# A graph network on one core: the first team's source slots sorted by readiness, 64 columns gathered ahead of a round's last stores, and the node groups in another order

## The chip, the cores and the metric

One core of one Trainium2 chip. The metric is the device time of one execution in microseconds (us). Engine names as in the profile: PE (TensorE matmul), PEld (its weight load), DVE (VectorE), ACT (ScalarE), POOL (GpSimd), SP (SyncE, which here only issues DMAs and passes semaphores on).

## The reference, cut to what matters

6250 nodes, 106250 edges sorted by target; the last edge of each node is its own loop. Three rounds of a mixture of experts (MoE) over the mean of the neighbours, then two attention layers (GAT) over the same edges.

```
h = x @ W_in + b_in                                   # 6250 x 256
for l in range(3):                                    # MoE rounds
    agg = segment_sum(h[src], dst) / deg
    logits = concat([h, agg]) @ router_W[l] + router_b[l]
    gates = softmax over the top 2 of 8 experts
    weak = relu(agg @ weak_W[l] + b)                  # 4 experts, 256 x 256
    strong = relu(agg @ strong_W1[l] + b) @ strong_W2[l] + b   # 4 experts, 256 x 512 x 256
    h = h + sigmoid(h @ conf_W[l] + conf_b[l]) * sum_e gates[e] * experts[e]
x = layernorm(x + h @ W_out + b_out)
x = layernorm(x + gat(elu(gat(x))))                   # softmax over each node's edges, 4 heads, then 1
```

A round cannot read h[src] of a node before the round before it has stored that node's new h.

## The kernel before, in words

**Groups, slots, teams.** Nodes are ranked by degree, the highest first, and cut into 49 groups of 128 (one node per partition). A group is as wide as its highest degree: that many *slots*, or columns. Column c of a group is one gathered row per partition. The 798 columns of all groups stand in one list (filled up to 800). Four groups are a team; 12 teams and a last one of one group. Which rank-group comes where is set by `rank_i`: group (rank-group + 1) * 12 mod 49. With the inputs of the reference this makes the teams 44, 62, 79, 69, 62, 75, 60, 61, 75, 56, 59, 74 and 22 columns wide (worked out from the drawn edges by the kernel's own rule).

**Gathering (POOL).** Per column POOL issues one indirect DMA (L591) of 128 rows of `hidden_tab[r]` (MoE rounds, 1 KB a row) or `gat_tab` (attention) into `ring`, a buffer of 32 columns. The row numbers are in `stage`, which SP loads by 32 columns. Four columns are a unit. SP waits for each unit's DMAs (L418) and raises `arrived`; DVE raises `ring_free` as it consumes a unit, and POOL waits for that before it writes over it. At the end of a round POOL waits for `table_done`, all 13 stores of the new h (L617).

**Summing and the MoE (DVE, PE, ACT).** `aggregate(r, q, j)` on DVE sums a group's columns: the first unit masked (L884), whole units added (L890), the last masked (L894), own row (L898), four slots to one (L901), times 1/degree (L905). In `step(q)` DVE sums the four groups of team q+1 between the pieces of team q: `rank_experts`, `weigh_experts`, `add_weak` (L934, L938) and `add_strong` (L925). PE begins team q by transposing its four sums (L1655, which waits for `agg_ready`), then runs router, strong and weak experts. ACT takes the results out of PSUM. `add_strong` of the last strong expert raises `h_done`; ACT then stores the team (`keep_state`, L1380). So a team's step on PE can begin when all columns of the team have come and been summed and PE is through with the team before.

**Between rounds.** After the last team, PE and ACT make the own part of the router's logits for all teams (L1633, L1644, L1307), and SP loads the next round's weights, after the first 32 columns of the round have come and PE's last strong expert is done (L443 to L448).

**Round 0** also notes for each gathered row where its node stands in the sorted order (`note_places`, L862), from which the list `place_tab` for all later rounds is made.

## Time and profile before

| | |
|---|---|
| median of 3 runs | 5833.66 us (5831.72 to 5834.1) |
| span of the profiled execution | 5830.9 us; no other time of it is recorded |
| busy: PE, PEld, DVE, ACT, POOL | 3215.0, 2026.1, 3413.5, 1201.4, 4155.7 us |
| first gather of MoE rounds 0, 1, 2 | 304.12, 1416.55, 2521.92 us |
| first gather of attention layers 1, 2 | 3698.28, 4739.33 us |

The span is 2.8 us below the median of the runs. Times in rows are us from the span's start. A gather counts as busy for its 0.95 us on POOL; the 0.30 us between two gathers is POOL's own issue time and shows as idle "<-issue".

### The profile page before, as it was taken

How to read it: one execution, taken by the hardware profiler on the slowest of the kernel's cores; microseconds unless marked ns; L12 is line 12 of the kernel's file. 1: busy time of each engine (PE TensorE's matmuls, PEld its weight loads, DVE VectorE, ACT ScalarE, POOL GpSimd, SP SyncE). 2: the span in 40 equal slices, each digit the busy share in tenths (PEclk: the TensorE clock that was granted, in tenths of full speed). 3: DMA queues.
4: the chain of work that ended last, by engine and by line, in shares of the span. 5: the costliest groups of instructions: out<-in, count | busy, mean ns of one | idle time of the engine just before them, and what ended most of it. 6: DMA issues, size and time to landing. Idle time of an engine off the chain costs nothing.

```text
span 5830.9 us, 59667 instructions
## 1 busy us (share of the span) xinstructions
PE 3215.0 (55%) x11995; PEld 2026.1 (35%) x11995; DVE 3413.5 (59%) x6741; ACT 1201.4 (21%) x2737; POOL 4155.7 (71%) x4323
## 2 busy tenths in 40 slices
PE   4088899999879899989899999200000000000000
PEld 3064555557545555565565566200000000000000
DVE  3255766773657666536566665555565556566563
ACT  1022323333223333323333333200000000000000
POOL 7777777772777777557777766477777767777777
PEclk8579999998889999979999999655555555555555
DMA  4244444441443333233333332222222222222221
GB/s 110 78 138 108 113 113 110 109 109 49 144 108 111 110 109 109 80 114 105 101 104 99 103 96 65 56 59 59 59 59 59 59 46 55 55 56 56 55 56 50
DMA packets 249575, 500.72 MB, mean 86 GB/s; under 512 B 104203, under 2 KB 133444, under 8 KB 249050
## 3 DMA queue, kind: packets, MB, share of 16 engines
q0 software_dynamic: 176592, 446.04, 29.6%
q1 hardware_dynamic: 56234, 33.56, 2.2%
q10 hardware_dynamic: 16608, 19.67, 0.9%
q14 instruction: 105, 0.86, 0.1%
q8 instruction: 36, 0.59, 0.0%
HBM read 464.21 MB, written 34.76 MB: 86 GB/s over the span
## 4 chain that ended last, share of the span: by engine, by line
POOL 25%; PE 22%; issue 16%; DVE 14%; DVEq 13%; DMA 5%; ACT 2%; SPq 1%; ACTq 0%; POOLq 0%
POOL ring L591 22%; PE ps_w1a L1681 4%; PE ps_w1b L1681 4%; PE ps_gate L1706 3%; DMA ring<-gat_tab,stage 3%; PE ps_wide L1706 3%; DVE ps_wide L1139 3%; PE ps_weak_a L1693 2%; PE ps_weak_b L1693 2%; DMA ring<-hidden_tab,stage 2%; DVEq L887 2%; DVE ps_wide L934 2%; DVEq L1171 1%; DVEq L1181 1%; DVEq L1184 1%
## 5 line engine op out<-in xcount | busy, mean ns | idle before, releaser
L591 POOL DMA_INDIRECT ring<-hidden_tab,stage x2400 | 2306.3, 961 | 955.5 <-issue 889.6
L591 POOL DMA_INDIRECT ring<-gat_tab,stage x1600 | 1539.3, 962 | 589.4 <-issue 545.5
L890 DVE TENSOR_TENSOR ps_wide<-ps_wide,ring 128x1024 f32<-128x1024 f32 x450 | 557.8, 1240 | 209.1 <-SPq L418 125.4
L1681 PE MATMUL ps_w1a<-agg_team_t,wbuf 128*128 128x512 f32 (+1 forms) x1248 | 561.6, 572 | 7.3 <-ACT strong L1347 5.9
L1706 PE MATMUL ps_gate<-wbuf,strong 128*128 128x256 f32 x2400 | 559.9, 379 | 0.0
L1810 PE MATMUL ps_w1a<-ident,agg_team_t 128*128 128x128 f32 x28 | 7.8, 434 | 995.0 <-DVE agg_team_t L1217 995.0
L1681 PE MATMUL ps_w1b<-agg_team_t,wbuf 128*128 128x512 f32 (+1 forms) x1248 | 556.0, 568 | 0.0
L1706 PE MATMUL ps_wide<-wbuf,strong 128*128 128x256 f32 x2304 | 537.2, 379 | 0.0
L1706 PEld LDWEIGHTS ps_gate<-wbuf,strong 128*128 128x128 f32 x2400 | 432.6, 190 | 111.2 <-issue 47.7
L1499 ACT ACTIVATE ps_gate<-shifted 128x36 f32<-128x36 f32 x296 | 60.4, 204 | 1859.3 <-DVEq L1128 1846.0
L1706 PEld LDWEIGHTS ps_wide<-wbuf,strong 128*128 128x128 f32 x2304 | 415.3, 190 | 78.5
L1145 DVE TENSOR_REDUCE h_res<-ps_wide 128x1188 f32 (+1 forms) x296 | 410.9, 1388 | 0.1
L934 DVE TENSOR_REDUCE ps_wide<-weak 128x256 f32<-128x1024 f32 x147 | 285.0, 1939 | 184.8 <-ACT weak L1368 168.8
L1139 DVE TENSOR_TENSOR ps_wide<-ring,ps_gate 128x1056 f32<-128x1056 f32 x296 | 372.9, 1260 | 0.0
L1347 ACT ACTIVATE strong<-ps_w1a,b_t 128x512 f32<-128x512 f32 (+1 forms) x312 | 206.8, 663 | 743.7 <-PE ps_w1a L1681 743.7
L1810 PEld LDWEIGHTS ps_w1a<-ident,agg_team_t 128*128 128x128 f32 x28 | 5.0, 216 | 997.1 <-DVE agg_team_t L1217 997.1
L894 DVE SCALAR_TENSOR_TENSOR ps_wide<-ring,before_cut,ps_wide 128x256 f32<-128x256 f32 x588 | 246.7, 485 | 177.4 <-SPq L418 138.0
L1681 PEld LDWEIGHTS ps_w1a<-agg_team_t,wbuf 128*128 128x128 f32 x1248 | 229.3, 190 | 307.3 <-issue 297.2
L1681 PEld LDWEIGHTS ps_w1b<-agg_team_t,wbuf 128*128 128x128 f32 x1248 | 231.5, 190 | 275.5 <-issue 275.5
L1111 DVE TENSOR_TENSOR score<-ring,h_res 128x32 f32 (+1 forms) x296 | 57.0, 193 | 437.2 <-SPq L422 381.3
L1693 PE MATMUL ps_weak_a<-wbuf,agg_team_t 128*128 128x512 f32 x588 | 288.1, 614 | 0.0
L1693 PE MATMUL ps_weak_b<-wbuf,agg_team_t 128*128 128x512 f32 x588 | 277.8, 595 | 0.0
(353 smaller groups left out, 4501.6 us busy)
## 6 DMA issues: line engine op xcount, KB each, us to landing
ring<-hidden_tab,stage POOLq DMA_INDIRECT x2400, 2.8
ring<-gat_tab,stage POOLq DMA_INDIRECT x1600, 2.6
hidden_tab<-h_res ACTq DMA_DIRECT2D x24, 512.0 KB, 3.0
hidden_tab<-h_res SPq DMA_DIRECT2D x12, 512.0 KB, 8.1
wbuf<-in_L_gnn_strong_W SPq DMA_DIRECT2D x6, 1024.0 KB, 10.1
wbuf<-in_L_gnn_strong_W SPq DMA_DIRECT2D x12, 512.0 KB, 13.7
gat_tab<-h_res ACTq DMA_DIRECT2D x7, 476.0 KB, 3.7
gat_tab<-h_res ACTq DMA_DIRECT2D x12, 272.0 KB, 2.4
```

The costliest lines, as they stand in the source:

```text
L591: return pool.indirect_dma_start(out=ring[:, b, 0:width], out_offset=None, in_=table, in_offset=bass.IndirectOffsetOnAxis(ap=stage[:, half ...
L887: dve.drain()
L890: nc.vector.tensor_tensor(wide_s, wide_s, rows(u), ALU.add).then_inc(ring_free, 1)
L894: nc.vector.scalar_tensor_tensor(wide_s[:, b, :], slot(last, b), before_cut[:, bass.ds(g + 1, 1), b:b + 1].rearrange("p a s -> p (a s)"), ...
L934: nc.vector.tensor_reduce(wide[:, 0:H], weak[j % 2][:].rearrange("p e n -> p n e"), AX.X, ALU.add)\
L1139: last = nc.vector.tensor_tensor(terms[:, 0:GSLOTS, :, :], rows_of(unit)[:, :, 0:HEADS * HC].rearrange("p s (h c) -> p s h c", c=HC), p[:, ...
L1145: nc.vector.tensor_reduce(sums(g), terms.rearrange("p s h c -> p (h c) s"), AX.X, ALU.add)
L1347: nc.scalar.activation(strong[s % 2][:, c, 0:size * P], ps_w1[c % 2][:, 0:size * P], ACT.Relu, bias=b1_t[:, k:k + 1]).then_inc(relu_ready, 1)
L1499: nc.scalar.activation(ps_gate[:, 0:(GSLOTS + 1) * HEADS], shifted[:].rearrange("p s h -> p (s h)"), ACT.Exp).then_inc(p_ready, 1)
L1681: last = mm(ps_w1[c % 2][:, 0:size * P], w1_w[:, k, s, c * P:(c + 1) * P], agg_team_t[:, k, 0:size * P], start=k == 0, stop=k == 1)
L1693: last = mm(ps_weak[x][:], agg_team_t[:, k, j * P:(j + 1) * P], wk_w[:, k, x * 512:(x + 1) * 512], start=False, stop=k == 1)
L1706: last = mm(o, strong[s % 2][:, c, j * P:(j + 1) * P], w2_w[:, c, s, :], start=False, stop=c == 3)
```

## The change

It does four things.

1. **Order of groups.** The four widest rank-groups become team 0; the other 45 are spread with a stride of 41, so that each team has wide and narrow groups. The teams are then 104, 69, 55, 57, 59, 59, 61, 61, 64, 64, 65, 67 and 13 columns wide; the sum stays 798, the list 800.
2. **Layout of the tables.** A node's row in `hidden_tab[1..2]` and `gat_tab` is (group, partition) in place of (partition, group), with one blank row between the first 11 teams and the last two, so that the rows of the last two teams are all above `BLANK`. A store of a team therefore writes four pieces per partition (1 KB, or 544 B in `gat_tab`) in place of one; the second `gat_tab` is stored in pieces by team.
3. **Sorting (once, in round 0, before team 6's step).** `count_late`, `sort_cells` and `place_parts` on DVE, with a transpose and three small matmuls on PE and two loads and one store of 224 columns on ACT, put the slots of team 0's nodes in order of their rows' place in the table. The 104 columns then are four *early* parts (rows below `BLANK` only), 26, 17, 15 and 14 wide with these inputs, and four *late* parts of 8 (worked out from the drawn edges as the kernel does; at most 8 sources of a node of team 0 lie in the last two teams). Where this arrangement is not possible, `apart` is 1 and two bodies of 32 blank columns are put ahead of the plain list; its conditions are met by these inputs.
4. **Rounds 1 and 2.** POOL gathers the first 64 columns once the first 11 teams are stored (`table_early`) and the rest after the last two (`table_late`). DVE sums early parts 0 and 1 inside the step of team 11 of the round before, parts 2 and 3 after the last team's last add, and the late parts at the start of the round. SP tells 64 columns before it loads weights, in place of 32.

The core of the diff:

```diff
-            nc.vector.tensor_scalar(rank_i[:, 0, :], rank_i[:, 0, :], 1.0, float(STRIDE), ALU.add, ALU.mult)
+            nc.vector.tensor_scalar(rank_i[:, 2, :], rank_i[:, 0, :], float(-TEAM), 0.0, ALU.add, ALU.max)
+            nc.vector.tensor_scalar(table_row, rank_i[:, 0, :], float(-TEAM), 0.0, ALU.add, ALU.min)
+            nc.vector.tensor_scalar(rank_i[:, 0, :], rank_i[:, 2, :], float(SPREAD), None, ALU.mult)
...
+                if 0 < r < LAYERS:                      # POOL
+                    table = whole[0:BLANK + 1, :]
+                    pool.wait_ge(table_early, 16 * (BATCHES - LATE_TEAMS) * r)
+                    rows(0, 0)
+                    rows(0, 1)
+                    table = whole
+                    pool.wait_ge(table_late, 16 * LATE_TEAMS * r)
-                if r < LAYERS - 1:
-                    pool.wait_ge(table_done, 16 * BATCHES * (r + 1))
+                if r == 0:
+                    pool.wait_ge(turned, 1)
+                    apart = pool.value_load(apart_i[0:1, 0:1], min_val=0, max_val=1)
...
                     tell(0)                             # SP
                     if r:
+                        load(2, 0, head)
+                        tell(1)
                         sp.wait_ge(w2_ready, r * BATCHES * 2 * NS)
...
+            def early_part(r, j):                       # DVE
+                part_units(r, j)
+                add_slots(early_sum[:, j, :])
+                dve.drain()
+            def late_part(r, j):
+                part_units(r, TEAM + j)
+                nc.vector.tensor_tensor(wide[:, H:2 * H], wide[:, H:2 * H], early_sum[:, j, :], ALU.add)
+                return mean_of(j, r * BATCHES, j)
...
                     spare = list(meanwhile)             # DVE, step
+                    if after == 1:
+                        add_strong(r, q - 1, NS - 1, TEAM)
                     gather_next(0)
...
                             add_weak(r, q, s, size)
+                        if after == 1 and s > 1 and r < LAYERS - 1:
+                            dve.drain()
+                            early_part(r + 1, s - 2)
...
-                    done = aggregate(r, 0, j)
+                    done = late_part(r, j) if r else aggregate(r, 0, j)
...
-                with dve.Fori(1, TEAMS - 1) as q:
+                with dve.Fori(1, TEAMS - 1 if r else TURN_AT) as q:
                     step(q, TEAM, TEAM)
+                if r == 0:
+                    dve.drain()
+                    count_late()
+                    sort_cells()
+                    apart = place_parts()
+                    with dve.Fori(TURN_AT, TEAMS - 1) as q:
+                        step(q, TEAM, TEAM)
...
                 add_strong(r, TEAMS, NS - 1, 1)
+                if r < LAYERS - 1:
+                    early_part(r + 1, 2)
+                    early_part(r + 1, 3)
...
                     for k in range(2):                  # ACT, step
                         take_agg_t(r, q, size, k)
+                    soon = after < TEAM and r < LAYERS - 1
+                    if soon:
+                        keep_state(r, q - 1, TEAM, late=after == 0)
                     logits_t(r, q, size)
...
+                    pe.wait_ge(late_counted, 1)         # PE, before team 6 of round 0
+                    nc.tensor.transpose(ps_sum[0:TEAM, 0:P], late4, ident[:]).then_inc(late_turned, 1)
+                    pe.wait_ge(late_known, 1)
+                    mm(ps_tr[:, 0:9], early_w.to_broadcast([TEAM, P]), above[:, 4:13], start=True, stop=False)
+                    mm(ps_tr[:, 0:9], late_w.to_broadcast([TEAM, P]), above[:, 0:9], start=False, stop=True)
+                    mm(ps_tr[:, 9:10], over.to_broadcast([TEAM, P]), above[:, 12:13], start=True, stop=True).then_inc(parts_placed, 1)
```

What stands where, in program order. First POOL at the end of round 0 (ring is the buffer, hidden_tab the table, ISA a bare wait or semaphore instruction). Before:

```order
L591 DMA ring<-hidden_tab,stage 128x257 [waits ring_free]
L591 DMA ring<-hidden_tab,stage 128x257
L620 ISA
L620 COMPARE_AND_BRANCH
L617 UNCONDITIONAL_BRANCH [waits table_done]
L617 ISA
L591 DMA ring<-hidden_tab,stage 128x256 [waits staged0]
```

and after the change:

```order
L659 DMA ring<-hidden_tab,stage 128x257 [waits ring_free]
L659 DMA ring<-hidden_tab,stage 128x257
L700 ISA
L700 COMPARE_AND_BRANCH
L713 TENSOR_LOAD apart_i [waits turned]
L713 ISA x2
L668 ISA [waits table_early]
L659 DMA ring<-hidden_tab,stage 128x256 [waits staged0]
L659 DMA ring<-hidden_tab,stage 128x256
```

The wait for all stores has become one for the first 11 teams; the wait for `table_late` now stands 64 gathers further on.

DVE in the step of team 11, round 0, from the second strong expert's add on (x_res, scaled_d: a scaled expert; weak: the weak experts' output). Before:

```order
L925 TENSOR_TENSOR h_res<-h_res,x_res 128x1024 [waits mo_copied]
L934 TENSOR_REDUCE ps_wide<-weak 128x256 [waits weak_copied]
L938 TENSOR_TENSOR h_res<-h_res,ps_wide 128x256
L925 TENSOR_TENSOR h_res<-h_res,x_res 128x1024 [waits mo_copied]
L934 TENSOR_REDUCE ps_wide<-weak 128x256 [waits weak_copied]
L938 TENSOR_TENSOR h_res<-h_res,ps_wide 128x256
L925 TENSOR_TENSOR h_res<-h_res,scaled_d 128x1024 [waits mo_copied]
L944 TENSOR_TENSOR logit<-logit,x_res 128x9 [waits logits_copied]
```

and the same place after the change, where the first rows of early part 0 stand between the second and the third add:

```order
L1141 TENSOR_TENSOR h_res<-h_res,x_res 128x1024 [waits mo_copied]
L1150 TENSOR_REDUCE ps_wide<-weak 128x256 [waits weak_copied]
L1154 TENSOR_TENSOR h_res<-h_res,ps_wide 128x256
L1015 TENSOR_LOAD x_res
L1015 ISA x2
L1016 TENSOR_LOAD x_res
L1016 ISA x2
L968 TENSOR_SCALAR from_cur<-x_res 128x4
L970 ISA
L973 ISA [waits arrived]
L973 TENSOR_SCALAR ps_wide<-ring,from_cur 128x256
```

A second early part stands in the same way between the last `add_weak` and the add of the last strong expert.

ACT in the step of the last team, round 0. After the change it reads as follows; the DMA (the store of team 11) with its wait for `h_done` is new at this place, and all that follows, the last team's logits first, is queued behind it:

```order
L1587 ACTIVATE scaled_d<-ps_wide,gates 128x256
L1552 ACTIVATE agg_team_t<-ps_w1a 128x128 [waits tr_ready]
L1552 ACTIVATE agg_team_t<-ps_w1b 128x128 [waits tr_ready]
L1611 DMA hidden_tab<-h_res 128x4x256 [waits h_done]
L1557 ACTIVATE logit_t<-ps_weak_a,rt_bias 9x128 [waits lgT_ready]
```

Before, that store stood further on, behind the first scaled strong expert of the last team.

## Rows read from the trace of the kernel before

**Rows 1.** The page: span, busy time, the chain that ended last

```profile
span 5830.9 us, 59667 instructions
...
POOL ring L591 22%; PE ps_w1a L1681 4%; PE ps_w1b L1681 4%; PE ps_gate L1706 3%; DMA ring<-gat_tab,stage 3%; PE ps_wide L1706 3%; DVE ps_wide L1139 3%; PE ps_weak_a L1693 2%; PE ps_weak_b L1693 2%; DMA ring<-hidden_tab,stage 2%; DVEq L887 2%; DVE ps_wide L934 2%; DVEq L1171 1%; DVEq L1181 1%; DVEq L1184 1%
```

**Rows 2.** Windows, gathers alone: stretch, length, POOL busy (count), PE clock, DMA share, GB/s

```profile
304.00:1327.00 1023.00, 770.25 (x800) 0.93 0.43 114
1416.00:2433.00 1017.00, 767.96 (x800) 0.93 0.39 114
2521.00:3557.00 1036.00, 768.10 (x800) 0.95 0.37 107
3698.00:4711.00 1013.00, 767.66 (x800) 0.50 0.27 58
```

**Rows 3.** Timeline of POOL at round ends: start, duration, instruction, idle before it

```profile
304.12 0.94 POOL L591 DMA_INDIRECT ring<-hidden_tab,stage  x1 [9.78 <-issue]
...
1416.55 0.94 POOL L591 DMA_INDIRECT ring<-hidden_tab,stage  x1 [90.82 <-issue]
```

**Rows 4.** Timeline of PE: first transposes of a team's step

```profile
372.99 1.09 PE L1655 MATMUL ps_w1a<-ident,x_res 128*128 128x128 f32 x4 [11.09 <-DVE x_res L905]
1308.63 1.09 PE L1655 MATMUL ps_w1a<-ident,x_res 128*128 128x128 f32 x4 [10.94 <-DVE x_res L905]
1485.29 1.09 PE L1655 MATMUL ps_w1a<-ident,x_res 128*128 128x128 f32 x4 [19.49 <-DVE x_res L905]
2009.16 0.60 PE L1655 MATMUL ps_w1a<-ident,x_res 128*128 128x128 f32 x4
2086.09 0.60 PE L1655 MATMUL ps_w1a<-ident,x_res 128*128 128x128 f32 x4
2413.46 1.09 PE L1655 MATMUL ps_w1a<-ident,x_res 128*128 128x128 f32 x4 [5.70 <-DVE x_res L905]
2949.32 0.60 PE L1655 MATMUL ps_w1a<-ident,x_res 128*128 128x128 f32 x4
3031.34 0.60 PE L1655 MATMUL ps_w1a<-ident,x_res 128*128 128x128 f32 x4
3537.74 0.63 PE L1655 MATMUL ps_w1a<-ident,x_res 128*128 128x128 f32 x4 [0.73 <-DVE x_res L905]
```

**Rows 5.** Timeline of DVE: ends of teams 11 and 12, rounds 0 and 1

```profile
1373.68 0.42 DVE L938 TENSOR_TENSOR h_res<-h_res,ps_wide 128x256 f32<-128x256 f32 x1
...
1388.91 1.22 DVE L925 TENSOR_TENSOR h_res<-h_res,scaled_d 128x1024 f32<-128x1024 f32 x1 [4.90 <-ACT scaled_d L1356]
...
1413.21 0.43 DVE L925 TENSOR_TENSOR h_res<-h_res,scaled_d 128x256 f32<-128x256 f32 x1 [2.31 <-ACT scaled_d L1356]
...
2518.63 0.43 DVE L925 TENSOR_TENSOR h_res<-h_res,scaled_d 128x256 f32<-128x256 f32 x1 [2.31 <-ACT scaled_d L1356]
```

**Rows 6.** Timeline of DVE: one group's sum in round 1

```profile
1486.11 0.17 DVE L879 TENSOR_SCALAR from_cur<-before_cut 128x4 f32<-128x4 f32 x1 [0.96 <-issue]
1486.64 1.65 DVE L884 TENSOR_SCALAR ps_wide<-ring,from_cur 128x256 f32 x4 [0.36 <-issue]
...
1490.21 1.23 DVE L890 TENSOR_TENSOR ps_wide<-ps_wide,ring 128x1024 f32<-128x1024 f32 x1 [0.34 <-issue]
1493.30 1.66 DVE L894 SCALAR_TENSOR_TENSOR ps_wide<-ring,before_cut,ps_wide 128x256 f32<-128x256 f32 x4 [1.86 <-SPq L418]
```

**Rows 7.** Timeline of ACT: the last team's logits in round 0

```profile
1389.82 0.36 ACT L1326 ACTIVATE logit_t<-ps_weak_a,rt_bias 9x128 f32<-9x128 f32 x1 [0.61 <-PE ps_weak_a L1665]
```

**Rows 8.** Timeline of DVE: small dependent operations of the gates

```profile
1247.24 0.20 DVE L966 RECIPROCAL gate_n<-gate_n 128x8 f32<-128x8 f32 x1
1247.51 0.17 DVE L968 TENSOR_TENSOR gate_n<-gate_n 128x4 f32<-128x4 f32 x1
```

**Rows 9.** The page, DMA issues: count, KB each, median us to landing

```profile
hidden_tab<-h_res ACTq DMA_DIRECT2D x24, 512.0 KB, 3.0
hidden_tab<-h_res SPq DMA_DIRECT2D x12, 512.0 KB, 8.1
```

More of the change, by code:

```diff
@@ L66 @@
 BATCHES = TEAMS + 1
-STORES = 2 * BATCHES + BATCHES
+STORES = BATCHES
+LATE_TEAMS = 2
+SOON = (BATCHES - LATE_TEAMS) * TEAM
+BLANK = SOON * P
+CELL = 40
+KEPT = 224
+FIRST_CALL = 2 * RING
+LEAD = FIRST_CALL // SLOTS
 SROWS = 64
@@ L72, with pieces_of @@
 EARLY = (TEAMS - 1) * TEAM
+TURN_AT = 6
+def pieces_of(b):
+    groups = range(b * GBATCH, (b + 1) * GBATCH)
+    return [(q, [g for g in groups if g // TEAM == q]) for q in sorted({g // TEAM for g in groups})]
+PIECES = sum(len(pieces_of(b)) for b in range(GBATCHES))
 LOWEST = -1.5e38
@@ L408, in _, with load @@
                 table = place_tab if r else slot_tab
-                def load(m, half):
-                    return sp.dma_start(stage[:, half, :], table[:, bass.ds(m * RING, RING)]).then_inc(staged[half], 16)
+                if r == 1:
+                    sp.wait_ge(turn_kept, 16)
+                    apart = sp.value_load(apart_i[0:1, 0:1], min_val=0, max_val=1)
+                rounds_of = bodies + apart * 2 if 0 < r < LAYERS else bodies
+                before_r = bodies * r + apart * (2 * (r - 1)) if 0 < r < LAYERS else 0
+                head = turn_tab if 0 < r < LAYERS else table
+                def load(m, half, table=table):
+                    at = m * RING if table is not place_tab or r >= LAYERS else m * RING - apart * FIRST_CALL
+                    return sp.dma_start(stage[:, half, :], table[:, bass.ds(at, RING)]).then_inc(staged[half], 16)
                 def tell(m):
@@ L470, in _ @@
                     continue
-                with sp.Fori(1 if r < LAYERS else 0, bodies // 2) as j:
+                turned_halves = KEPT // RING // 2 if r < LAYERS else 0
+                if r < LAYERS:
+                    with sp.Fori(1, turned_halves) as j:
+                        load(j * 2 + 1, 1, head)
+                        tell(j * 2)
+                        load(j * 2 + 2, 0, head)
+                        tell(j * 2 + 1)
+                with sp.Fori(turned_halves, rounds_of // 2) as j:
                     load(j * 2 + 1, 1)
@@ L505, in _ @@
                                     base=-1, pattern=[[-1, P]], channel_multiplier=1)
+            nc.gpsimd.affine_select(out=above[:], in_=above[:], compare_op=ALU.is_gt, fill=0.0,
+                                    base=-TEAM, pattern=[[1, 13]], channel_multiplier=-1)
             nc.gpsimd.memset(wrap[0:1, P - 1:P], 1.0)
@@ L605, in attention_rows @@
                     i = bodies * (r - LAYERS) + j * 2 + half
-                    pool.wait_ge(staged[half], loads[half] * (16 * r) + j * 16 + 16)
+                    pool.wait_ge(staged[half], loads[half] * (16 * r) + more + j * 16 + 16)
                     pool.sem_inc(half_begun, 1)
@@ L900, in aggregate @@
                 dve.drain()
-                nc.vector.tensor_reduce(part[:], wide.rearrange("p (s n) -> p n s", n=H), AX.X, ALU.add)
+                add_slots(part[:])
                 dve.drain()
@@ L1409, in step @@
                         take_state(r, q - 1, TEAM)
-                    elif tail:
+                    elif tail and not soon:
                         keep_state(r, q - 1, TEAM)
```

259 lines of the change are left out of this document (206 added, 53 removed).

## The prediction

> **What bounds the kernel now.** I read the page first: POOL is the busiest engine, and its gathers head the chain that ended last with 22% [rows 1]. Then the windows on the gathers alone. Every round issues 800 of them and takes 1017 to 1036 us for it, 1.27 to 1.28 us a gather; the 0.95 us of the gather and 0.30 us of issue come to 1.25 [rows 2, 3]. So POOL has next to no stall inside a round, in the attention layers too. What is left is between the rounds: POOL stands idle for 90.8 us before round 1 [rows 3], and as long before round 2, because it waits for the last store.
>
> The timeline of PE says how far the rest could follow a faster POOL. Where PE finds its sums ready, it begins a team every 76.9 us in rounds 0 and 1 and every 82.0 us in round 2, which also projects the output (2086.09 - 2009.16; 3031.34 - 2949.32) [rows 4]. POOL brings an average team (798 / 12.25 = 65 columns) in 83 us. So PE lies just below the bound: it waited 10.94 us for the sums of team 11 in round 0, 5.70 in round 1 and 0.73 in round 2 [rows 4]. What the change gives POOL beyond some 6% of a round, PE will not pass on.
>
> I measure a round from T, the end of the last add of the round before: 1413.64 and 2519.06 [rows 5]. PE begins team 0 at T + 71.7 (1485.29), team 11 at T + 999.8 in round 1 (2413.46) and T + 1018.7 in round 2 (3537.74) [rows 4]. From team 11's begin to the last add it is 105.0 us in round 0 (1413.64 - 1308.63) and 105.6 in round 1. The first gather follows T by 2.9 us [rows 3, 5].
>
> **Round 0: the wide team goes first and nothing is gathered ahead.** PE began team 0 at 372.99, 68.9 us after the first gather; team 0 then needed 12 units, 48 columns. 48 x 1.277 = 61.3, so 7.6 us, say 8, pass from the last gather's issue to the sums. After the change team 0 needs units 0 to 26, 108 columns: 304.1 + 138 + 8 = 450, a begin 77 us later. Team 1 needs 176 columns: 304.1 + 225 + 8 = 537. From then on PE at 77.3 us a team (my value between 76.9 and the 79.2 of 1308.63 to 1387.84) is behind POOL: team 11 begins at 537 + 773 = 1310 by PE, and by POOL at 304.1 + 788 x 1.277 + 8 = 1318. The loss of 77 us is thus made good almost wholly, since the teams behind are even and 1308.63 was POOL's pace.
>
> Into this comes the sorting on DVE, between two steps. I count 18 register loads, 31 dependent stages, and 9 stages of four MAX or MATCH_REPLACE each. Two loads and what goes with them leave 0.96 us [rows 6], so 18 x 0.48 = 9; a small stage is 0.27 us [rows 8], so 8; 6 for the 9 stages (estimate: some 0.1 us more than a small stage for each of four); 3 for the two loads of 224 columns, near ACT's 3.0 us for a store [rows 9]; 1.5 for two exchanges with PE. Together 27 us. DVE has 3 us of slack a team, so little is made good that way, but PE can go on for part of it with work whose sums are there: I pass on 18 of the 27 to PE. Bounds: 0 (all covered) and 27. By PE team 11 begins at 1328, by POOL at 1318. Two paces so near each other disturb each other; I take 1334. **Round 0: +25 us**, bounds 8 and 40.
>
> **The ends of rounds 0 and 1: what the early parts push back.** DVE finishes the third weak expert at 1374.1, and the fourth team-wide add was at 1388.91 [rows 5]. In between now stands early part 0: 26 columns, first unit, five whole ones, last. By one group's rows [rows 6]: 0.96 + 0.17 + 0.36 + 1.65 to the end of the first unit, 5 x (1.23 + 0.34), then 0.34 + 1.66 and a reduction of 1.3: 14.5 us, to 1388.7. Then an add (1.3), the fourth weak sum (2.5), and part 1 (17 columns, three whole units, 11.3 us): 1404. The add of the last strong expert ends at 1405.4, 15.3 us later than 1390.1. ACT's store of team 11, which the order puts ahead of the last team's logits, waits for just that. The logits stood at 1389.82 [rows 7] and now come at some 1406. Router, experts and gates of the last team are queued behind them, each waiting for the other engine, so all of it moves: **+16 us in each of two rounds, 32 in all**. Bounds 8 (if waits inside the last team shrink) and 20.
>
> Do the 64 columns come in time? POOL ends round 0 some 13 us after team 11's begin B, and the store of team 10 is out by then. The first 30 columns go into free slots; the next waits for DVE to take early unit 0, at about B + 69. The 34 left need 43 us: B + 113, and T is at B + 121. So they are hidden. Parts 0 and 1 need column 43 at most, which comes at B + 87, before part 1 begins at B + 85 plus its first units.
>
> The stores are now pieces of 1 KB. The row for such pieces, SP's stores in the preparation, has 8.1 us to landing against ACT's 3.0 with 4 KB pieces [rows 9]. That does not matter for MoE rounds: the store of team 11 is issued 15 us ahead of T, and the last one has one group and had 1 KB pieces already. The Trainium skill, "DMA: Bandwidth & Descriptors", section Specifications, has transfers at line rate from 512 B on; by that rule the finer stores would cost nothing at all, and the row with 8.1 us, taken beside other traffic, neither bears it out nor refutes it. In the attention layers the last batch goes out as three DMAs with 544 B pieces, on the path: between 0 and 5.1 us (8.1 - 3.0), I take **+3**. Some more small operations in the preparation: **+1** (four stages of 0.27).
>
> **Rounds 1 and 2: what is gained.** At T + 2.9 POOL goes on with column 64. Team 0 needs column 107: 44 x 1.27 = 56, and with 8 of sums T + 67 to 68, against T + 71.7. Here alone nearly nothing comes of it, since team 0 is now 104 wide in place of 44. (DVE's parts 2 and 3, 11 us each, and three late parts of 9.6 us end before that.) The gain is in the POOL timeline after it, 64 - (104 - 44) columns and even teams behind. Team 1 needs 176 columns: T + 2.9 + 112 x 1.27 + 7 = T + 152. Team 11 by POOL: T + 2.9 + 724 x 1.27 + 7 = T + 929. By PE in round 1: 152 + 10 x 77.3 = T + 925; I take T + 935, since the two are equal: **-65 us** against T + 999.8. Bounds -70 and -45 (81.5 us a team in place of 77.3 plus what they cost each other). In round 2 PE decides: 152 + 820 = 972, I take T + 975: **-44 us** against T + 1018.7. Bounds -47 and -25.
>
> After round 2 nothing changes on the path; the attention layers stay at POOL's pace, 1.27 us a gather [rows 2], whatever the order of the groups.
>
> **Sum:** 25 + 32 + 3 + 1 - 65 - 44 = -48 us. On the span: 5830.9 - 48 = 5783; the median of the runs is 2.8 us above the span, so 5786 us. A measurement of this kernel can tell some 0.2% (12 us) from no change.
>
> **Rivals.**
>
> *A. The small gain (18%).* The sorting passes on in full (+27 in place of 18), and teams in rounds 1 and 2 keep 3 us of mutual waits each. For it: three engines of nearly one pace. -48 + 9 + 2 x 10 + some waits = -15: about 5818.
>
> *B. The large gain (16%).* The ends are not pushed back, because DVE's idle time there takes the early parts, and PE covers the sorting. For it: DVE is idle for 4.90 us ahead of the add at 1388.91. Against it: part 0 alone is 14.5 us. -48 - 20 - 18 = -86, about 5748.
>
> *C. Slower (6%).* The early columns come late: POOL waits for ring slots until DVE takes them, and DVE in turn waits in part 0 for `arrived`, in the middle of team 11's step. Each us of that is paid in both rounds, since the last team is queued behind. It decides from 24 us a round on (48 / 2). If POOL's call began 40 us later than I have it, the result would be +32: 5866. Against it: the store of team 10 needs only that team's last add, which DVE now does first in team 11's step, and 3.0 us to land [rows 9], while POOL is busy with round 0 until B + 13 anyway.
>
> *D. It doesn't do what it says (4%).* If `apart` came out as 1, 64 blank columns would be gathered ahead and nothing real: team 0 at T + 147, team 11 at T + 1011, that is +11 in both rounds in place of the gains. 25 + 32 + 4 + 22 = +83: 5917. Against it: by the drawn edges the early parts are 72 wide, and 64 are needed.
>
> *E. No change (3%).* Gains and losses of A grow together until within 12 us.
>
> **How the numbers follow.** The sum has 53%; its own range is 5765 to 5806. Below it B, above it A, then C and D. Leaving out the outer half of B and all of C and D, the range is 5738 to 5826. Faster by over 0.2% (below 5822): the sum's 53, B's 16 and 15 of A's 18, 84%. Within 0.2%: the rest of A, E, and one of C: 7%. Slower: 9%.
>
> **What would show it.** POOL's idle time ahead of round 1 falls from 90.8 us to under 10, and a new one of some 10 us stands 30 columns later, one of 5 to 15 us 64 columns later. PE begins team 0 of round 0 near 450 and team 11 near 1334; from there to the last add it takes 121 us in place of 105. From T, team 0 begins at 67 to 68, team 11 at 935 and 975. PE has a wait of some 10 us ahead of team 6 in round 0, and one inside team 6 or 7. Wrong would be: gathers slower than 1.28 us in the rounds, a round 0 whose loss is not made good (team 11 beyond 1350), or last teams that are not pushed back.

## The result, and the profile after

The changed kernel takes 5844.2 us, the kernel before 5835.2 us on the same chip: a ratio of 1.0015, 95% interval 1.0008 to 1.0021. It is slower by 0.15%: the interval leaves out 1, and the difference is less than the 0.2% that the prediction took as what can be told from no change. Forecast were 5786 us, a range of 5738 to 5826, and chances of 0.84 for faster and 0.07 for within 0.2%. Run once more beside other kernels it was at 1.0016 (1.0006 to 1.0026). The profiled executions differ by 10.0 us.

The page of the changed kernel: span, the lines of the chain, the queue that fetches instructions for the engines, the stores:

```profile
span 5840.9 us, 59986 instructions
...
q14 instruction: 109, 0.89, 0.0%
...
PE 31%; POOL 24%; issue 15%; DVE 10%; DVEq 10%; DMA 5%; ACT 1%; ACTq 0%; POOLq 0%; SPq 0%
POOL ring L659 21%; PE ps_w1a L1924 6%; PE ps_w1b L1924 6%; PE ps_gate L1949 5%; PE ps_wide L1949 5%; DMA ring<-gat_tab,stage 3%; PE ps_weak_a L1936 3%; DVE ps_wide L1370 3%; PE ps_weak_b L1936 3%; DVEq L976 1%; DMA ring<-hidden_tab,stage 1%; PE ps_weak_a L1908 1%; DVE ps_wide L1150 1%; DVEq L1402 1%; DVEq L1412 1%
...
hidden_tab<-h_res ACTq DMA_DIRECT2D x24, 512.0 KB, 3.3
hidden_tab<-h_res SPq DMA_DIRECT2D x12, 512.0 KB, 7.6
```

The windows from the first to the last gather of rounds 0, 1 and 2 and of the first attention layer, to be laid beside [rows 2]: stretch, length, busy time (count) of PE, PEld, DVE, ACT and POOL, granted PE clock, DMA share, GB/s.

```profile
304.00:1382.00 1078.00, 918.65 (x3196) 568.72 (x3241) 682.18 (x1426) 301.32 (x621) 774.54 (x800) 0.90 0.41 109
1390.00:2452.00 1062.00, 998.88 (x3574) 621.52 (x3622) 688.65 (x1245) 335.12 (x703) 770.74 (x800) 0.95 0.38 110
2458.00:3548.00 1090.00, 1039.29 (x3879) 659.01 (x3926) 683.09 (x1238) 358.25 (x740) 778.19 (x800) 0.96 0.36 102
3699.00:4716.00 1017.00, 31.77 (x126) 27.45 (x126) 586.48 (x1221) 50.17 (x218) 767.65 (x800) 0.51 0.25 58
```

POOL at the begin of round 1: first gather, the 31st, the 65th, each with its wait:

```profile
1389.82 0.95 POOL L659 DMA_INDIRECT ring<-hidden_tab,stage  x1 [7.27 <-DMA stage<-turn_tab]
...
1448.25 0.95 POOL L659 DMA_INDIRECT ring<-hidden_tab,stage  x1 [21.21 <-DVE ps_wide L973]
...
1508.85 0.95 POOL L659 DMA_INDIRECT ring<-hidden_tab,stage  x1 [17.61 <-issue]
```

What the change promises it does. The 90.8 us ahead of round 1 [rows 3] have gone to 7.3, with the two smaller waits behind. But 800 gathers of round 0 now take 1078 us where 1023 were enough, though POOL is busy for only 4 us longer (774.5 for 770.3 us): it waits for free slots of the ring, that is for DVE. From the begin of team 2 to that of team 11, POOL waits 1.5 to 10.8 us a step for DVE (29.7 us in the one behind the sorting), and DVE waits only 0.6 to 1.8 us a step for columns. In the last three of these steps in round 1 DVE waits 4.0 to 7.0 us for columns: there POOL is the slower one.

PE at the begins of teams 0, 5, 6 and 11 of round 0, of team 0 of round 1, of its team 4 (no wait), team 11 of round 1 and of round 2, and the wait inside the last team of round 0:

```profile
444.60 1.08 PE L1898 MATMUL ps_w1a<-ident,x_res 128*128 128x128 f32 x4 [83.22 <-DVE x_res L998]
...
856.72 0.66 PE L1898 MATMUL ps_w1a<-ident,x_res 128*128 128x128 f32 x4 [2.68 <-DVE x_res L998]
962.09 0.60 PE L1898 MATMUL ps_w1a<-ident,x_res 128*128 128x128 f32 x4
...
1379.23 1.08 PE L1898 MATMUL ps_w1a<-ident,x_res 128*128 128x128 f32 x4 [6.25 <-DVE x_res L998]
...
1476.58 1.22 PE L1924 MATMUL ps_w1a<-agg_team_t,wbuf 128*128 128x128 f32 x4 [15.99 <-ACT strong L1578]
...
1570.43 1.08 PE L1898 MATMUL ps_w1a<-ident,x_res 128*128 128x128 f32 x4 [13.91 <-DVE x_res L998]
...
1888.05 0.60 PE L1898 MATMUL ps_w1a<-ident,x_res 128*128 128x128 f32 x4
...
2443.19 1.09 PE L1898 MATMUL ps_w1a<-ident,x_res 128*128 128x128 f32 x4 [6.73 <-DVE x_res L998]
...
3542.26 0.60 PE L1898 MATMUL ps_w1a<-ident,x_res 128*128 128x128 f32 x4
```

The end of the last addition is T = 1501.97 in round 0 and 2566.76 in round 1. The terms of the sum stand beside each other:

| | before | forecast | after |
|---|---|---|---|
| round 0: team 0 begins | 373.0 | 450 | 444.6 |
| round 0: team 11 begins | 1308.6 | 1334 (+25) | 1379.2 (**+70.6**) |
| team 11 to last addition, rounds 0, 1 | 105.0, 105.6 | 121 (+16 each) | 122.7, 123.6 (+17.7, +18.0) |
| T to team 0, round 1 | 71.7 | 67 to 68 | 68.5 |
| T to team 11, round 1 | 999.8 | 935 (-65) | 941.2 (-58.6) |
| T to team 11, round 2 | 1018.7 | 975 (-44) | 975.5 (-43.2) |
| all else | | +4 | +5.5 |

"All else" is the rest of the 10.0 us between the spans. All terms but one are within 7 us of the forecast. Round 0 alone is off, by 46 of the 58 us of the error.

### The profile page after: what moved, and what is told of

Read it like the earlier page. It is cut to its first block, busy times and chain, and to the rows that moved or that the text cites. A ratio compares the mean times of both kernels' runs of the same rounds, so it can differ in the third digit from the quotient of the medians.

```text
span 5840.9 us, 59986 instructions
## 1 busy us (share of the span) xinstructions
PE 3204.8 (55%) x11855; PEld 2033.3 (35%) x12002; DVE 3455.5 (59%) x6929; ACT 1201.4 (21%) x2737; POOL 4179.1 (72%) x4326
## 3 DMA queue, kind: packets, MB, share of 16 engines
q0 software_dynamic: 176592, 446.04, 29.2%
## 4 chain that ended last, share of the span: by engine, by line
PE 31%; POOL 24%; issue 15%; DVE 10%; DVEq 10%; DMA 5%; ACT 1%; ACTq 0%; POOLq 0%; SPq 0%
POOL ring L659 21%; PE ps_w1a L1924 6%; PE ps_w1b L1924 6%; PE ps_gate L1949 5%; PE ps_wide L1949 5%; DMA ring<-gat_tab,stage 3%; PE ps_weak_a L1936 3%; DVE ps_wide L1370 3%; PE ps_weak_b L1936 3%; DVEq L976 1%; DMA ring<-hidden_tab,stage 1%; PE ps_weak_a L1908 1%; DVE ps_wide L1150 1%; DVEq L1402 1%; DVEq L1412 1%
## 5 line engine op out<-in xcount | busy, mean ns | idle before, releaser
L983 DVE SCALAR_TENSOR_TENSOR ps_wide<-ring,before_cut,ps_wide 128x256 f32<-128x256 f32 x556 | 231.3, 484 | 128.2 <-SPq L472 76.1
L973 DVE TENSOR_SCALAR ps_wide<-ring,from_cur 128x256 f32 x620 | 255.7, 481 | 39.5 <-issue 36.5
```

The source lines that it names most:

```text
L973: taken = nc.vector.tensor_scalar(wide_s[:, b, :], slot(first, b), from_cur[:, b:b + 1], None, ALU.mult)
L983: nc.vector.scalar_tensor_tensor(wide_s[:, b, :], slot(last, b), ended(b), wide_s[:, b, :], ALU.mult, ALU.add)
```

## Why round 0: what DVE does there

DVE in team 8's step of round 0, which is the begin of a loop pass, and then at the same place of the program in round 1 (team 4's step):

```profile
1139.06 0.17 DVE L968 TENSOR_SCALAR from_cur<-before_cut 128x4 f32 x1 [4.87 <-issue]
1139.72 0.17 DVE L955 COPY spots<-ring  x1 [0.49 <-issue]
1139.85 1.65 DVE L973 TENSOR_SCALAR ps_wide<-ring,from_cur 128x256 f32 x4
1141.99 0.26 DVE L955 COPY spots<-ring  x1 [0.49 <-issue]
1142.12 1.26 DVE L979 TENSOR_TENSOR ps_wide<-ps_wide,ring 128x1024 f32<-128x1024 f32 x1
1143.85 0.17 DVE L955 COPY spots<-ring  x1 [0.48 <-issue]
1143.98 1.23 DVE L979 TENSOR_TENSOR ps_wide<-ps_wide,ring 128x1024 f32<-128x1024 f32 x1
...
1893.65 0.20 DVE L968 TENSOR_SCALAR from_cur<-before_cut 128x4 f32 x1 [1.60 <-issue]
1894.20 1.65 DVE L973 TENSOR_SCALAR ps_wide<-ring,from_cur 128x256 f32 x4 [0.35 <-issue]
1896.20 1.23 DVE L979 TENSOR_TENSOR ps_wide<-ps_wide,ring 128x1024 f32<-128x1024 f32 x1 [0.35 <-issue]
```

Two things are dearer in round 0. A unit takes 1143.98 - 1142.12 = 1.86 us, against 1.57 in rounds without the noting copy (1.23 + 0.34 in [rows 6]); over all units of round 0 it is some 0.28 us a unit. And the first instruction behind the loop's jump comes after an idle 4.87 us in place of 1.60, with "issue", not another engine, as its cause.

The sorting, on DVE: the last operation ahead of it, its first, one of the copies behind two register loads, its last but some; and PE's wait for its first result:

```profile
944.25 0.42 DVE L1154 TENSOR_TENSOR h_res<-h_res,ps_wide 128x256 f32 x1 [0.20 <-issue]
944.79 0.11 DVE L1033 MEMSET x_res<- 128x64 int32 x1
...
965.91 0.18 DVE L1112 COPY x_res<-x_res  x1 [1.47 <-issue]
...
972.04 0.39 DVE L1117 TENSOR_TENSOR x_res<-x_res 128x224 int32<-128x224 int32 x1
```

```profile
950.01 0.37 PE L2015 MATMUL ps_wide<-ident,x_res 128*4 128x128 f32 x1 [22.30 <-DVEq L1052]
```

It is 28 us long (944.79 to 972.97), as forecast (27). The step from the begin of team 5 on PE to that of team 6, in which it falls, takes 105.4 us, its neighbours 80.7 and 84.5.

Theory 1, from these rows: DVE paces round 0 of the changed kernel. Noting, loop edges (the idle time behind a loop's jump) and sorting lie in series on an engine without slack there, while the kernel before had round 0 paced in the main by POOL, whose 83 us a team hid the noting and the edges. The rivals: the sorting alone does it (it stalls PE and POOL and they don't catch up), or the new order of the columns does it, or the round's begin. The last is out by the table: team 0 begins at 444.6. TensorE's clock is out as well: from team 0's begin on it was granted at 0.95 (444 to 958 us), 0.96 (to 1100) and 0.97 (to 1382), and the 0.90 of the whole window comes from 0.50 before team 0, while PE stood waiting.

## Experiments

Times are medians; the ratio is to the kernel before on the same chip, with its 95% interval. The changed kernel stands at 1.0016. The difference of two ratios times 5835 gives microseconds; with intervals of 0.001 to 0.0017 on each side it is good to some 8 to 12 us, so smaller steps are read from the traces.

**e1 and e2: the noting copy left out from team 3 of round 0 on**, in the changed kernel and in the one before (the rows' places are then not noted, and later rounds gather other rows; as many of them).

```
+                if r == 0:
+                    with dve.Fori(1, 2) as q:
+                        step(q, TEAM, TEAM)
+                noting[0] = False              # note_places does nothing from here
...                                            # the loop over the teams goes on from team 2
```

> The changed kernel, round 0 without the noting of places (the COPY to spots) from team 3 on; the list for the later rounds keeps old entries from there, so it leaves out part of the computation. Theory 1 (DVE paces round 0 once team 0 is the wide one): teams 3 to 11 of round 0 begin every 77 to 78 us in place of 82.5, team 11 near 1335 in place of 1379, total 40 to 45 us below the changed kernel, that is about 5800. Theory 2 (round 0 is slow for another reason: the PE clock after the sorting, or POOL): under 10 us, 5835 to 5845.

> The kernel before, with the same part of the noting left out (so it leaves out part of the computation). Theory 1: before, round 0 was paced by the gathers (team 11 cannot begin before column 776 is there), so DVE's saving is worth 0 to 8 us: 5827 to 5835. Theory 2 (DVE paced round 0 before as well): 25 us or more.

Measured: e1 5806.9 us, 0.9958 (0.9941 to 0.9975), 34 us less than the changed kernel, where 40 to 45 were expected. e2 5827.8 us, 0.9997 (0.9988 to 1.0007): no difference. The same copies are free before and dear after. Team 11 of round 0 begins at 1344.4 in e1 (1379.2; 1335 was expected). In its last three steps, 80.7 to 85.9 us, DVE waits 4 to 10 us for columns: once DVE is quicker, POOL paces them. And a part of the gain was not the copy: in the second loop of round 0 the edge fell with it from 5.0 to 1.62 us, and one long edge of the first loop fell from 6.8 to 1.9 us. The run does not part the two.

**e3: no sorting.** The edges of the parts are constants, and the list of team 0 is the unsorted one, in which the blank row stands for every row of the last two teams (the minimum below). PE's part of the sorting is left out too. As many rows are gathered, of which some are wrong; everything else is as in the changed kernel.

```
-                    count_late()
-                    sort_cells()
-                    apart = place_parts()
+                    nc.vector.tensor_scalar(turn_cols, kept_cols[...], float(BLANK), None, ALU.min)
...
+                    apart = 0
...
```

> The changed kernel without the sorting: the bounds of the eight parts are constants, the first 224 columns are taken over with one minimum against the blank row, so part of the sources are wrong rows; everything else is the same. Theory 1 (DVE is the pace of round 0, so the sorting is paid in full): team 6 to team 7 of round 0 falls from 105 us to about 82, total 22 to 27 us below the changed kernel, about 5819. Theory 2 (my prediction's way, two thirds passed on, the rest covered): 18 us, 5826. Theory 3 (covered): under 8 us.

Measured: 5807.9 us, 0.9962 (0.9948 to 0.9976), 32 us less, where at most 27 were expected. The sorting's own step fell from 105.4 to 80.3, 25 us, and teams 0 to 11 of round 0 together took 897.1 us (1340.50 - 443.38) for 934.6. Beside the sorting's step it is again the loop edges that differ, of loops in which nothing was changed. The edge of e3's loop in round 0, then that of its loop in round 1:

```profile
854.10 0.30 DVE L969 TENSOR_SCALAR from_cur<-before_cut 128x4 f32 x1 [1.62 <-issue]
...
1861.62 0.17 DVE L969 TENSOR_SCALAR from_cur<-before_cut 128x4 f32 x1 [6.24 <-issue]
```

In the changed kernel it is the other way round: 6.5 to 6.8 us in round 0's first loop, 4.9 to 5.0 in its second, 1.6 in round 1. The 6.2 us in e3's round 1 cost next to nothing: PE begins teams 2 to 7 there every 76.7 to 77.3 us, and teams 0 to 11 take 875.9 us, for 875.0 and 875.3 with short edges in e1 and e10.

**e4: the order of columns alone**, in the kernel before: nothing gathered ahead, no sorting.

```
-            nc.vector.tensor_scalar(rank_i[:, 0, :], rank_i[:, 0, :], 1.0, float(STRIDE) ...
+            nc.vector.tensor_scalar(rank_i[:, 2, :], rank_i[:, 0, :], float(-TEAM), 0.0, ALU.add, ALU.max)
+            ...                                   # as in the changed kernel
```

> The kernel before with nothing but the new order of the groups (team 0 104 columns wide). Theory 1: round 0 pays 45 to 50 us (start 72 us later, partly made good), rounds 1 and 2 begin team 0 at T + 147 in place of T + 72; team 11 then at T + 1003 to 1011 in round 1 (+3 to +11) and T + 1053 in round 2 (+34); total +85 to +100, about 5925 to 5935; the gather ahead is then worth some 115 us less the sorting and the pushed-back ends. Theory 2 (the gather ahead moves little, since PE paces rounds 1 and 2): order alone is within 30 us of the changed kernel, 5840 to 5870.

Measured: 5926.4 us, 1.0164 (1.0147 to 1.0181). Alone the order costs 97 us; gathering ahead, with the sorting's price taken off, gives back all but 9 of them. The total is what theory 1 said, not every term of it: team 11 of round 1 begins at T + 1020.4, 20.6 us later than before, where 3 to 11 were expected. POOL and PE at the begin of round 1 of e4, with a full pause and 104 columns before the first team:

```profile
1458.32 0.94 POOL L592 DMA_INDIRECT ring<-hidden_tab,stage  x1 [104.49 <-issue]
```

```profile
1599.10 1.09 PE L1660 MATMUL ps_w1a<-ident,x_res 128*128 128x128 f32 x4 [94.56 <-DVE x_res L910]
```

From T to team 0 it is 143.7 us in e4 and 68.5 in the changed kernel: 75 us a round, the worth of gathering ahead. Team 0 to team 11 of round 0 takes 908.1 us in e4, so without any sorting, against the 884 of the forecast, of which 18 were for sorting: the forecast of round 0 was off before the sorting came to it.

**e10: DVE's two loops over the teams of round 0 written out.**

```
-                with dve.Fori(1, TEAMS - 1 if r else TURN_AT) as q:
-                    step(q, TEAM, TEAM)
+                if r: ...                         # the loop, as it was
+                else:
+                    for q in range(1, TURN_AT):
+                        step(q, TEAM, TEAM)
...                                               # the second loop in the same way
```

> The changed kernel, with VectorE's two loops over the teams of round 0 (teams 1 to 5, and 6 to 10) written out team by team; the other engines and rounds keep their loops. In the changed kernel VectorE stands idle 6.5 to 6.8 us at each edge of the first loop and 4.9 to 5.0 us at each edge of the second, and 1.6 us at those of round 1. Theory 1 (VectorE paces teams 1 to 5, and the gathers of 64 columns teams 7 to 10): the steps of teams 1 to 5 fall from 81.5 us on average to 79 or 80, those behind the sorting stay at 82 to 84; team 11 begins 8 to 15 us sooner and the whole takes 5830 to 5837. Theory 2 (VectorE has slack in round 0 but for the sorting): within 3 us of the changed kernel. Theory 3 (straight code waits for instructions all along): 10 us slower or more.

> The changed kernel as it is, run beside the others for a difference taken on the same chip: 5840 to 5850 by the earlier measurement of 5844, with team 11 of round 0 again at 1379 and the steps of teams 1 to 5 between 79 and 84 us if they are a matter of the code and not of that one execution.

Measured: e10 5820.0 us, 0.9984 (0.9975 to 0.9994); the changed kernel beside it (e12) 5838.5 us, 1.0016. 18.5 us less, where 8 to 15 were expected. (e12 was expected at 5840 to 5850; the kernel before is 5.7 us quicker on this chip than in the first measurement, and the ratio is as it was.) In e12 team 11 begins at 1380.4 and the four steps from team 1 to team 5 are 80.7 to 82.6 us, so they are a matter of the code. In e10 they are 77.0 to 79.3, and those behind the sorting fell too (mean 83.5 to 82.3): only at team 11, for which PE waits 10.8 us and DVE 9.6 us for columns, is POOL the slower one. PE at team 11 of round 0 in e3, then in e10:

```profile
1340.50 1.09 PE L1910 MATMUL ps_w1a<-ident,x_res 128*128 128x128 f32 x4 [5.57 <-DVE x_res L999]
```

```profile
1354.70 1.09 PE L1901 MATMUL ps_w1a<-ident,x_res 128*128 128x128 f32 x4 [10.81 <-DVE x_res L998]
```

The begin of a step in e10, its idle time 0.88 us, and e10's line of the instruction queue:

```profile
847.01 0.17 DVE L968 TENSOR_SCALAR from_cur<-before_cut 128x4 f32<-128x4 f32 x1 [0.88 <-issue]
```

```profile
q14 instruction: 84, 0.69, 0.0%
```

**e5, e6, e7: three single repairs elsewhere; e8: all three.** e5 puts ACT's store of team 11 back behind the last team's first strong expert. e6 moves early part 0 ahead of a weak sum and part 1 ahead of a strong addition. e7 shifts the ranks by one, so that team 1 takes 55 columns where it had 57 and the teams after it grow slowly.

```
-                    soon = after < TEAM and r < LAYERS - 1          # e5
+                    soon = after == 1 and r < LAYERS - 1
...
+                        if after == 1 and s == 2 and r < LAYERS - 1:  # e6, ahead of add_weak(r, q, s)
+                            dve.drain()
+                            early_part(r + 1, 0)
...                                                     # part 1 likewise at s == 3, ahead of add_strong
-            nc.vector.tensor_scalar(rank_i[:, 2, :], rank_i[:, 0, :], float(-TEAM), 0.0, ALU.add, ALU.max)     # e7
+            nc.vector.tensor_scalar(rank_i[:, 2, :], rank_i[:, 0, :], float(1 - TEAM), 0.0, ALU.add, ALU.max)
```

> The changed kernel, with one thing undone: at the end of rounds 0 and 1 ScalarE stores team 11's rows only behind the last team's first scaled strong expert, as in the kernel before, and not ahead of it (the order of ScalarE's queue alone; the early columns still follow the stores they need). In the changed kernel the stretch from the begin of team 11 to the last addition is 122.7 and 123.6 us in rounds 0 and 1, against 105.0 and 105.6 before, and TensorE stands idle 16 us before the last team's first turn. Theory 1 (the store stands ahead of an expert's scaling on ScalarE, and all of the last team hangs on that): each end gets some 7 us shorter, 14 us in all, so about 5830. Theory 2 (VectorE's early parts of round r+1, which stand ahead of the last team's sums, set the end, and ScalarE has slack): no more than 2 us an end, 5840 to 5845.

> The changed kernel, with VectorE's early parts 0 and 1 of the next round moved ahead by half a strong expert each at the end of rounds 0 and 1: part 0 ahead of the weak expert's addition of slot 2, part 1 ahead of the strong expert's of slot 2, places at which VectorE waits for TensorE anyway. Theory 1 (ScalarE's store sets the end): nothing or a few us, 5838 to 5845. Theory 2 (the parts stand ahead of the last team's sums and TensorE's idle 16 us is their time): some 10 us an end, 20 in all, about 5824.

> The changed kernel, with the next rank group put with team 1: the ranks are shifted by 1 - TEAM in place of -TEAM, so that team 1 takes 55 columns after team 0's 104, and the sizes grow slowly from there to 72 (104, 55, 57, 59, 59, 61, 61, 64, 64, 65, 67, 69, 13 for 104, 57, 57, 59, 59, ... as now). Theory 1 (TensorE's first turn of team 1 waits for the gathers of its columns, 86 us behind team 0's begin, and nothing behind it catches this up): each round's steps from team 0 to team 1 get 7 us shorter where TensorE paces what follows (rounds 1 and 2), less in round 0, which VectorE paces: 15 to 22 us in all, 5822 to 5830. Theory 2 (the ring is full or VectorE paces, so a gain at team 1 is waited away by team 11): within 3 us of the changed kernel, 5841 to 5847.

> The three edits of the runs beside it together: ScalarE's store behind the last team's first strong expert, VectorE's early parts half an expert sooner, and the narrower team 1. Theory 1 (each wait is its own and the gains add up): the sum of the three single gains, 14 + 10 + 18 or some 42 us, about 5800. Theory 2 (the waits hide one another, so that the single edits gain little but together free the end of a round): the single runs sum to under 15 us, and this one gains over 25. Theory 3 (VectorE's pace of round 0 takes back what is won there): 25 to 30 us, 5815 to 5820.

| | us | ratio (interval) | less than 1.0016 | team 11 to last addition |
|---|---|---|---|---|
| e5 | 5828.4 | 0.9992 (0.9982 to 1.0001) | 14 us | 114.7, 114.3 |
| e6 | 5824.0 | 0.9982 (0.9973 to 0.9992) | 20 us | 112.4, 113.8 |
| e7 | 5826.2 | 0.9987 (0.9978 to 0.9997) | 17 us | 123.4, 122.0 |
| e8 | 5791.8 | 0.9928 (0.9911 to 0.9944) | 51 us | 104.7, 103.6 |

Theory 1 of e5 and theory 2 of e6 both held, although each was the other's rival: the 16 us of PE's idle time in the last team had two causes in a row. The early parts delay the addition, and the store that waits for it delays the last team's logits and all that ACT has behind them. DVE and ACT there, in the changed kernel:

```profile
1474.17 1.22 DVE L1141 TENSOR_TENSOR h_res<-h_res,scaled_d 128x1024 f32<-128x1024 f32 x1
```

```profile
1475.47 0.39 ACTq L1611 DMA_DIRECT2D hidden_tab<-h_res  x1
1475.91 0.36 ACT L1557 ACTIVATE logit_t<-ps_weak_a,rt_bias 9x128 f32<-9x128 f32 x1 [16.99 <-DVEq L1143]
```

and ACT in e5, where the logits go first:

```profile
1459.57 0.36 ACT L1557 ACTIVATE logit_t<-ps_weak_a,rt_bias 9x128 f32<-9x128 f32 x1 [0.61 <-PE ps_weak_a L1908]
...
1478.59 0.39 ACTq L1611 DMA_DIRECT2D hidden_tab<-h_res  x1
```

The single gains of e5, e6 and e7 add up to 51 us, and e8 gains 51, where 42 were expected. The ends of rounds 0 and 1 are back at 104 to 105 us with early parts 0 and 1 in them: their summing was hidden wholly, so that the +16 of each end was a matter of their place.

**e9: team 0 of 96 columns, with e8's edits** (rank groups 5, 6, 7 in place of 1, 2, 3), **and e11: e9 and the loops written out.**

> The three edits together (store behind the first strong expert, parts half an expert sooner, narrow team 1), and team 0 made of other rank groups: groups 5, 6 and 7 stand in place of 1, 2 and 3, so that the sizes are 96, 55, 57, 59, 59, 61, 61, 64, 66, 66, 69, 72, 13 in place of 104, 55, 57, 59, 59, 61, 61, 64, 64, 65, 67, 69, 13; the 64 early columns stay, and the late ones are 32 in place of 40. Theory 1 (at each round's begin team 0 waits for 40 late columns at 1.25 us or so each, and PE paces what follows): team 0 begins 10 us sooner in each of three rounds, but the larger teams 8 to 11 (66 to 72 columns at 1.28 us, 84 to 92 us a team) give some of it back; 5770 to 5785, against 5792 for the three edits alone. Theory 2 (a round is paced by its whole count of 692 gathers, wherever they stand): team 11 begins as late as now, and the time stays at 5788 to 5796.

> All five edits of the runs beside and before it together: the store later, the parts sooner, the narrow team 1, the team of 96, and VectorE's loops of round 0 written out. If the gains add up, it takes what the team of 96 takes less what the written-out loops gain by themselves: 5760 to 5785 by theory 1 of both. If the larger late teams and the written-out loops meet (VectorE's gain is waited away, since the gathers pace the second half of round 0), no better than the team of 96 alone.

Measured: e9 5780.1 us, 0.9912 (0.9896 to 0.9929); e11 5771.7 us, 0.9903 (0.9886 to 0.9919), both inside the range of their theory 1. (e11's four runs, 5769.3 to 5774.6 us, lie just below e9's, 5774.7 to 5780.6.) The trace of e9 shows that its reason is half wrong. Round 0 ends 24 us sooner than in e8 (1458.3 for 1482.6), but round 1, from T to T, takes 8 us more (1053.7 for 1045.8) and round 2 takes 1.5 more: the larger teams 8 to 11 take back what the begin gives, as theory 2 had it. And of the 24 us, 12.5 are team 0's begin; 11 more came in the steps up to team 11, whose loop edges are now 1.6 us, in loops that were not edited. One of these edges in round 0, and e9's line of the instruction queue:

```profile
835.25 0.32 DVE L981 TENSOR_SCALAR from_cur<-before_cut 128x4 f32 x1 [1.60 <-issue]
```

```profile
q14 instruction: 69, 0.57, 0.0%
```

## Why the prediction was wrong, step by step

**The step that failed** is "DVE has 3 us of slack a team" and, with it, "From then on PE at 77.3 us a team" in round 0. In the changed kernel DVE has no slack in that round; it is the bound. The prediction gives no row for the 3 us. Its 76.9 us "in rounds 0 and 1" comes from a row of round 1, where DVE notes no places, and its 79.2 from round 0's last step, which stands outside the loop. Rows of the kernel before would have told: in round 0 the step from team 6 to team 7 took 80.1 us; at its end PE waited 3.0 us for DVE, and in it POOL waited 3.7 us for DVE.

```profile
898.80 0.60 PE L1655 MATMUL ps_w1a<-ident,x_res 128*128 128x128 f32 x4
978.89 0.65 PE L1655 MATMUL ps_w1a<-ident,x_res 128*128 128x128 f32 x4 [3.00 <-DVE x_res L905]
```

In e2, without the copy, the same step takes 76.9 us and PE doesn't wait, though DVE's loop edges are longer there (5.1 to 5.4 us for 4.1 to 4.4), so it was the copy:

```profile
895.96 0.60 PE L1661 MATMUL ps_w1a<-ident,x_res 128*128 128x128 f32 x4
972.89 0.60 PE L1661 MATMUL ps_w1a<-ident,x_res 128*128 128x128 f32 x4
```

From team 0 to team 11 the forecast has 884 us, the changed kernel 934.6; the prediction's own sign of being wrong, "team 11 beyond 1350", came true. The runs share the excess out. Round 1 needs 872.7 for the same teams (941.2 - 68.5); that is already 12.7 more than the forecast has without sorting and mutual waits (87 + 773 = 860), since POOL paces the last three steps, 80.7 to 85.2 us. e3, with noting but short edges and no sorting, needs 897.1: the noting costs 24 (21 beside e3's own round 1, 875.9). e10, with the sorting and no loop edges, 911.4: the sorting costs 14. The changed kernel, with its long edges, 934.6: these cost 23. The shares depend on the order in which they are taken, since the engine's slack is used up by whichever comes first (without sorting the long edges cost 11, 908.1 - 897.1, and the sorting beside them 26.5). Together they are 62 us; forecast were 18 for the sorting and 6 for two paces that disturb each other. So 12.7 + 62 - 24 = 50.7 us is what the forecast missed between teams 0 and 11. That the noting costs 24 rests on a comparison of round 0 in e3 with round 1 of the changed kernel, not on one edit.

**Round 0's other numbers** held: team 0 at 444.6 (450), team 1 at 531.0 (537), the sorting 28 us long (27). How much of it is passed on depends on what is compared: 25 of 28 us where its step is laid beside e3's, 14 to 26.5 over the whole round by the shares above, with 18 forecast. The prediction had PE go on with other work for a part of it; it could not: it stands at its place in the program for 22.3 us until DVE has come to the counting.

**The ends of the rounds** held: +17.7 and +18.0 for +16. The mechanism given, ACT's store ahead of the logits, is shown by e5, and by e6 that the place of the parts is its first cause. The prediction did not see that both could be moved at no cost; rival B's "ends are not pushed back" came true only in e8, where they are moved.

**Rounds 1 and 2** held: -58.6 for -65 within its bounds, -43.2 for -44. POOL's new waits stand where they were announced, but longer: 21.2 us (some 10 forecast) and 17.6 (5 to 15). Two readings in the prediction are off without a part in the miss: 1036 us for 800 gathers in round 2 is 1.30 us a gather, not 1.28, and early part 0 adds up to 14.3 us, not 14.5.

**GAT and preparation:** the stores in the attention layers were to cost 3. The pause between the layers did not grow (28.7 us, 29.2 before), so the finer stores cost nothing on that path; instead the 800 gathers of each layer took 4 to 6 us longer (1017.6 and 1021.6 for 1011.9 and 1017.6), in other runs of the new order 1014 to 1021. In the first layer POOL waits 7.1 us in four places for DVE to free the ring, where it waited 1.0 us before, which makes up the difference there; in the second layer no such wait accounts for the 4 us, and their cause is open. The rest of "all else" is a gain of 3.9 us at the end of round 2 (118.9 to 114.9 us from team 11 to the last addition). The Trainium skill, "DMA: Bandwidth & Descriptors", section Specifications, has line rate from 512 B on. The trace agrees to within 10%: MoE stores of 1 KB pieces landed in 3.3 us, those of 4 KB pieces before in 3.0 [rows 9].

**The rivals:** none named DVE as the new bound. Rival A had the three engines' nearness and the whole of the sorting, for 33 us; the first of these was too small. The time came out where E (3%) had it, by gains and losses that nearly cancel, but not by E's mechanism. C did not occur: in early parts 0 and 1 of round 0's end DVE waits for columns 0.3 us at a time, as long as its own issue. Nor did D: team 0 begins at T + 68.5, not T + 147. D's own sum was too small, for e4, which has its late begin, puts team 11 of round 2 32.9 us later than before, where D took 11.

## What to carry to other kernels

Where a change takes away the wait that paced a stage, read the slack of the other engines from that very stage, not from a sister stage with almost the same code: work that costs nothing under one bound (here a copy of 0.28 us a unit, e2) costs some 24 of its 48 us under the next (0.28 us by 170 units from team 1 to team 11; an estimate from the shares above). When two engines' instructions wait for one another in a row, repair them one by one and together; here the singles added up. And an experiment that takes out code can change loop edges elsewhere, as e1, e3 and e9 did, so compare the loop edges of both traces before a difference is put down to what was taken out.

## What the runs showed of the hardware

The idle time of DVE behind a loop's jump has levels: 1.6 us, or 4.1 to 7.0 us. It is within 0.6 us the same at all edges of one loop, and it changed with edits elsewhere. The kernel before has the long one in round 0 and the short one in round 1:

```profile
1229.23 0.17 DVE L879 TENSOR_SCALAR from_cur<-before_cut 128x4 f32 x1 [4.29 <-issue]
...
2012.33 0.17 DVE L879 TENSOR_SCALAR from_cur<-before_cut 128x4 f32 x1 [1.62 <-issue]
```

